# Rolled rows loaded with the 40 fields outermost, repeated rows written from SBUF, and k2 loaded last, in a DLRM tower on one core

## The reference, cut to what matters

```
e = stack([tbl_f[ids[:, f]] for f in range(40)], axis=1)      # (512, 40, 16)
x = e
for k in (k0, k1, k2):                                         # k0 (128, 40, 40), k1 and k2 (128, 128, 40)
    x = einsum('bhd,bmd,ohm->bod', x, e, k)                    # (512, 128, 16)
    outputs.append(sum(x, axis=-1))                            # (512, 128)
h = concatenate(outputs + [dense_ctx], axis=1)                 # (512, 384 + 16)
h = maximum(h @ W_top1 + b_top1, 0)                            # (512, 512)
h = maximum(h @ W_top2 + b_top2, 0)                            # (512, 256)
y = h @ W_top3                                                 # (512, 1)
```

## Time and profile before

| | |
|---|---|
| median of 3 runs | 780.76 us (780.18 to 788.1) |
| profiled execution | 787.09 us, of which the span of its instructions is 785.1 us |
| busy share, PE / DVE / ACT / POOL | 86% / 85% / 68% / 35% |
| mean granted TensorE clock | 0.972 |
| moved by DMA | 43.03 MB, 55 GB/s over the span |
| start of the first matmul on Y | 59.35 us |

### The profile page before, as it was taken

One profiled execution on the slowest core, in us unless ns is written; L12 is line 12 of the kernel. 1 busy time (PEld: TensorE's weight loads), 2 busy tenths in 40 slices (PEclk: granted clock), 3 DMA queues, 4 the chain that ended last, 5 costly groups with the idle time before them and its releaser, 6 DMA issues.

```text
span 785.1 us, 12097 instructions
## 1 busy us (share of the span) xinstructions
PE 672.4 (86%) x2558; PEld 479.5 (61%) x2558; DVE 670.2 (85%) x1607; ACT 530.8 (68%) x1753; POOL 274.8 (35%) x250
## 2 busy tenths in 40 slices
PE   0057998989888989898989999898989898987998
PEld 0025766666656767676756666666666676764483
DVE  3325999999979999999979999999999999999391
ACT  2204787868757777777766777786878687787293
POOL 6413244443533353535344444444353501010000
PEclk9997999999999999999989999999999999999699
DMA  6251212112211121212112111111211211100000
GB/s 193 58 183 56 60 63 48 59 53 56 57 53 45 41 63 51 58 44 66 45 55 45 64 46 62 47 57 52 60 52 48 61 50 55 51 1 28 0 1 1
DMA packets 45538, 43.03 MB, mean 55 GB/s; under 512 B 25615, under 2 KB 28943, under 8 KB 45216
## 3 DMA queue, kind: packets, MB, share of 16 engines
q1 hardware_dynamic: 40352, 41.07, 16.3%
q0 software_dynamic: 5120, 1.32, 2.7%
HBM read 41.06 MB, written 1.97 MB: 55 GB/s over the span
## 4 chain that ended last, share of the span: by engine, by line
PE 52%; DVE 25%; issue 10%; DMA 6%; ACT 3%; DVEq 2%; SPq 1%; POOL 1%; ACTq 0%
PE Y L610 10%; PE Y L612 10%; PE Y L611 10%; DVE sums L522 10%; PE X L577 7%; DVE sums L478 5%; DVE sums L483 5%; DMA pairs<-scratch 3%; PE GB L584 3%; DVE pairs_lo L455 3%; ACT sums L403 2%; DVE sums L469 2%; DMA scratch<-x0g 2%; PE X L571 2%; PE X L638 1%
## 5 line engine op out<-in xcount | busy, mean ns | idle before, releaser
L403 ACT ACTIVATE sums<-Y,xtok 128x128 f32<-128x128 f32 x1536 | 423.8, 380 | 125.8 <-PE Y L612 114.4
L610 PE MATMUL Y<-k1lo,x1hi 128*128 128x512 f32 x640 | 302.1, 472 | 29.6 <-DVE sums L522 22.0
L522 DVE SCALAR_TENSOR_TENSOR sums<-Y,xtok,sums 128x128 f32<-128x128 f32 x1024 | 285.8, 342 | 19.2 <-ACT sums L403 11.7
L611 PE MATMUL Y<-k1hi,x1hi 128*128 128x512 f32 x640 | 255.9, 400 | 0.0
L612 PE MATMUL Y<-k1hi,x1lo 128*128 128x512 f32 x640 | 255.7, 400 | 0.0
L338 POOL TENSOR_TENSOR diag<-xtok,mask 128x320 f32<-128x320 f32 x64 | 81.2, 1269 | 363.4 <-PE GB L584 363.2
L309 POOL DMA_INDIRECT x0g<-in_table,rows_now x160 | 189.3, 1183 | 42.2 <-issue 38.7
L610 PEld LDWEIGHTS Y<-k1lo,x1hi 128*128 128x128 f32 x640 | 122.2, 191 | 88.7 <-DVE sums L522 44.3
L611 PEld LDWEIGHTS Y<-k1hi,x1hi 128*128 128x128 f32 x640 | 122.8, 192 | 41.5 <-issue 14.4
L612 PEld LDWEIGHTS Y<-k1hi,x1lo 128*128 128x128 f32 x640 | 122.3, 191 | 30.3
L448 DVE TENSOR_TENSOR pairs<-pairs,A 120x512 f32<-120x512 f32 x112 | 76.6, 684 | 31.2 <-DMA pairs<-scratch 31.2
(11 more groups left out here) (74 smaller groups left out, 365.6 us busy)
## 6 DMA issues: line engine op xcount, KB each, us to landing
pairs<-scratch SPq DMA_DIRECT2D x112, 240.0 KB
A<-scratch SPq DMA_DIRECT2D x16, 240.0 KB
k1raw<-in_k SPq DMA_DIRECT2D x1, 2560.0 KB, 10.4
x0g<-in_table,rows_now POOLq DMA_INDIRECT x160, 3.8
k2s<-in_k SPq DMA_DIRECT2D x1, 2560.0 KB, 14.1
scratch<-x0g SPq DMA_DIRECT2D x64, 20.0 KB, 1.7
pairs<-in_w SPq DMA_DIRECT2D x3, 256.0 KB, 3.0
scratch<-scratch SPq DMA_DIRECT2D x16, 40.0 KB, 2.0
```

The costliest lines, as they stand in the source:

```text
L403: ins = nc.scalar.activation(sums[tile % 2][:, k * O:(k + 1) * O], Y[(NCH * tile + c) % YB][:, i * O:(i + 1) * O], ACT.Copy, scale=xtok[sl ...
L522: nc.vector.scalar_tensor_tensor(out=chain[tile % 2][:, i * O:(i + 1) * O], in0=Y[(NCH * tile + c) % YB][:, i * O:(i + 1) * O], scalar=xto ...
L610: nc.tensor.matmul(y, hi[:, tok], k1lo[:, cols], start=True, stop=False)
L611: nc.tensor.matmul(y, hi[:, tok], k1hi[:, cols], start=False, stop=False)
```

## The change

Three things are changed. First, the address pattern by which `A3` and `pairs` are loaded from `scratch` has the 40 fields outermost and the 3 shifts inside, instead of the other way round. A partition now is field x 3 + shift rather than shift x 40 + field; the host orders the rows of k0's weights accordingly, and `xtok` takes every third column of each token's transposed rows. Second, the rows 40 to 59 of `scratch` are written straight from `x0g` by two more transfers of 20 KB, in place of the copy of 40 KB in DRAM, and the wait between is gone. Third, SP issues the load of k2 behind its last group, not behind the first.

```
                 def rows(first, step):
                     return bass.AP(scratch.tensor, (par * ROLLS + first) * GROUP,
-                                   [[step * GROUP, KC], [GROUP, M], [1, GROUP]])
+                                   [[GROUP, M], [step * GROUP, KC], [1, GROUP]])
 
                 sp.wait_ge(s_gather[par], 16 * GF * (GPB // 2 * u + (slot + 1) // 2 + 1))
                 for q in range(FQ):
-                    sp.dma_start(scratch[par, q * GF:(q + 1) * GF, :].rearrange("f (b d) -> b f d", d=D),
-                                 x0g[par][q * GS:(q + 1) * GS, :, :]).then_inc(s_scratch, 16)
-                sp.wait_ge(s_scratch, 16 * FQ * (g + 1))
-                sp.dma_start(scratch[par, M:ROLLS, :], scratch[par, 0:ROLLS - M, :]).then_inc(s_again, 16)
-                sp.wait_ge(s_again, 16 * (g + 1))
+                    for first in range(q * GF, ROLLS, M):
+                        sp.dma_start(scratch[par, first:first + GF, :].rearrange("f (b d) -> b f d", d=D),
+                                     x0g[par][q * GS:(q + 1) * GS, :, :]).then_inc(s_scratch, 16)
+                sp.wait_ge(s_scratch, 16 * (ROLLS // GF) * (g + 1))
                 sp.dma_start(A3[par][0:PR, :], rows(0, 0)).then_inc(s_a3, 16)
...
             spread(0, -1)
-            sp.dma_start(k2s[:, :, :], k2.rearrange("h (m o) -> h m o", o=O)).then_inc(s_k2, 16)
-
             def body(u, last):
                 for slot in range(GPB - last):
                     spread(u, slot)
             over_groups(sp, body)
 
+            sp.dma_start(k2s[:, :, :], k2.rearrange("h (m o) -> h m o", o=O)).then_inc(s_k2, 16)
             sp.wait_ge(s_x1free, NG)
...
                     nc.scalar.activation(xtok[par][:, :, :], TR[:, 0:TPG * PR].rearrange(
-                        "p (j r) -> p j r", r=PR)[:, :, 0:M], ACT.Copy).then_inc(s_xtok, 1)
+                        "p (j m k) -> p j m k", m=M, k=KC)[:, :, :, 0], ACT.Copy).then_inc(s_xtok, 1)
...
     for k in range(KD):
-        k0a[k % KC, :, k // KC] = k0[h, (h + k) % M]
+        k0a[:, k % KC, k // KC] = k0[h, (h + k) % M]
         if 0 < k < KD - 1:
-            k0b[k % KC, :, k // KC] = k0[(h + k) % M, h]
+            k0b[:, k % KC, k // KC] = k0[(h + k) % M, h]
```

More of the change, by code:

```diff
@@ L208, in build @@
         s_xtok = sem("xtok_ready")
-        s_scratch, s_again, s_a3 = sem("scratch_written"), sem("scratch_repeated"), sem("a3_in")
+        s_scratch, s_a3 = sem("scratch_written"), sem("a3_in")
         s_roll = [sem(f"rolled_in{i}") for i in range(NR)]
@@ L679 @@
     h = np.arange(M)
-    k0a = np.zeros((KC, M, NC0, O), np.float32)
-    k0b = np.zeros((KC, M, NC0, O), np.float32)
+    k0a = np.zeros((M, KC, NC0, O), np.float32)
+    k0b = np.zeros((M, KC, NC0, O), np.float32)
     for k in range(KD):
-        k0a[k % KC, :, k // KC] = k0[h, (h + k) % M]
+        k0a[:, k % KC, k // KC] = k0[h, (h + k) % M]
         if 0 < k < KD - 1:
-            k0b[k % KC, :, k // KC] = k0[(h + k) % M, h]
+            k0b[:, k % KC, k // KC] = k0[(h + k) % M, h]
     ident, mask = constants()
```

## The result

The changed kernel took 759.8 us (758.94 to 760.03, 4 executions), the kernel before in the same set 784.43 (780.18 to 789.02, 4 executions). The ratio is 0.968, 95% interval 0.961 to 0.975: 3.2% faster. Repeated later with 6 executions beside 11 of the kernel before it was 759.9 against 781.56, ratio 0.970 (0.966 to 0.975). The forecast was 758.3 in a range of 752 to 767.

The account below looks back on a forecast made before the run. VectorE was taken to bound steady groups, leaving gains only at the start: 16.3 there plus 6.2 at group 1 gives 22.5 us, taking the median 780.76 to 758.3, range 752 to 767.

Parts of the forecast that it names:

- The bound: Steady groups: VectorE's own instructions set the 40.47 us period, loads cost nothing there, and groups stay at 40.5.
- Part 1: Start of group 0: forty fields outermost cut a load from 3.3 to 1.0 us; start gains 16.3, copy and k2 included.
- a chain of computing takes over from the loads: Group 0's start: with short loads, computing sets the time; product 0 at 27.6, first Y matmul at 43.0 us.
- xtok's stride: ScalarE reading every third element in PSUM: bounds 0 and 4.8 us per group, 0.3 at worst in group 0; taken as nothing.
- Part 2: SP's queue: copy's 2.07 us wait removed, two issues of 0.94 added; net 1.1 earlier, counted in group 0, hidden later.
- the price of small pieces: Scratch writes in 64-byte pieces: by the 512 B rule two more could cost about 1 us once, giving 21.5 gained.
- Part 3: k2 issued last: the 6.15 us wait at group 1's first product goes, gaining 6.2; no cost at the end.
- The sum: Whole kernel: 16.3 at the start plus 6.2 at group 1 gives 22.5 us, subtracted from the median 780.76.
- such a stall may come or not: Two loop edges: ScalarE's idle put down to issue, 10.3 us together, treated as occasional and left out of the gain.
- Rival 1: Loads not widened, descriptors still dealt three ways: only 9.3 us gained, giving 771.5; chance 0.05.
- Rival 2: TensorE granted clock 0.5 for all of group 0: 34 us over the period, giving 792.3; chance 0.03.
- Rival 3: More engines reading overlapping DRAM rows get worse than three: at 6 us a load, 113 us slower; chance 0.02.

Follow-up runs that it names:

- the kernel before with the move: Kernel before, with eight top-layer matmuls needing only z0 and the context put ahead of the last G on TensorE: 784.37 us.
- the pair with the move: Changed kernel and kernel before, each with eight top-layer matmuls put ahead of the last G: 755.16 and 784.37 us.
- the kernel with k2 and writes: Changed kernel with loads turned back to 3 shifts outermost, keeping k2 last and the two added writes: 777.64 us, 0.990 of the kernel before.

## Why the prediction was right, point by point

**The bound.** The steady group was set by VectorE and didn't move, 40.44 against 40.47. Right.

**Part 1, the width and the start.** A load takes 1.06 us; the forecast had 1.0. The first matmul on Y came at 41.91 where 43.0 was forecast, so 17.4 instead of 16.3. From the last matmul of chunks 0 to 2 to the product whose load waited for it took 3.5 to 3.8 us, where 3.5 was taken for the landing alone, so this term held. The two steps that were off: the A3 issue was at 21.68, not 22.25, since six writes from 17.41 landed in 4.27 us; and TensorE's rows had come to their higher level by 34.57, so that four matmuls take 2.25, where the forecast kept 2.99 from the earlier trace rows. TensorE then waits 0.65 and 0.70 us for products 5 and 6, so the landings decide the end of the chain. The reading that a chain of computing takes over from the loads is right in kind. Loads 4 to 6 remain in it with a wait of 1.1 us each. They were forecast to be on par with TensorE.

**xtok's stride** costs nothing: 304 ns against 303.

**Part 2.** By the last x1lo the writes gave 3.1 alone and 1.1 on top of k2's move (671.4 to 670.3), where 1.1 was forecast; both lie within the spread of that event. In group 0 A3's issue follows the first write by 4.27 us instead of 5.65, a gain of 1.4. Alone they also shorten the wait at group 1. The small pieces were no loss beside the copy: the writes' median time to landing stays 1.7 us, so the 1 us that the forecast gave as the price of small pieces did not show.

**Part 3.** Group 0 is 7.1 shorter, 6.2 of it forecast. Most of the rest, 0.7, is TensorE's clock at the first matmuls on Y. k2's move at the end cost nothing: it is issued at 634.3, lands in 8.8 us and is first read at 686.6.

**The sum** was 22.5, and 24.6 and 21.7 were measured by medians in the two sets. That it came so near is in part luck, as two errors cancel in it. The step that failed is "such a stall may come or not": the loop-edge waits belong to the three-wide loads and are worth 5.9 us, which the change gained beyond the forecast. Nor were these waits the 6.3 us between the profiled execution and the median: the kernels at 771 (span 769.2) and at 776.54 (the kernel before with the move) have both of them. What the 6.3 us were isn't shown. The stretch at clock 0.50 at the end is a part at most; in the profiled pair the end took 2.2 us more after the change, and no execution of the kernel before near 780 was profiled. Without the end, the change is worth 30.4 us in this pair of profiles and 29.2 in the pair with the move (678.6 to 649.4), while the medians of the kernels without the move show 24.6 and 21.7. This difference is only in part accounted for.

**The rivals.** Rival 1 (no widening) is what the kernel with k2 and writes is; its gain was priced at 9.3 and is 9.7 by the last x1lo, but 3.9 by its median (781.57 to 777.64). Rival 2 feared a lower clock in group 0; there it was granted 1.00 throughout (first windows above), more than the 0.85 before, which gave 0.7 us. The clock mattered more at the other end of the program. Rival 3 had no sign.

## What to carry to other kernels

Read the DMA share while a single transfer runs. Here a share near 3/16 stood beside an outermost dimension of 3, and 0.64 beside one of 40. Putting a larger dimension outermost is free if the order of partitions can be folded into the host's weights. The cost of a narrow load isn't only its own time: the narrow loads here were hidden in all steady groups and still cost 5.9 us, through another engine's wait at the loop edges. And when executions differ by 1% without a pattern, look at the granted clock at the end before explaining the difference by the change, and compare by an event ahead of it, knowing how far that event repeats (649.4 to 652.7 here).

## What the runs showed of the hardware that I had not expected

- A wait "<- issue" of 5 us on ScalarE behind a loop's branch follows the narrow traffic: twice in each of six profiles with it (five kernels with narrow loads and the one with narrow loads added), never in seven without. It ends 1.2 to 2.2 us after a packet of the instruction queue.
- In eleven of twelve profiles with a pause of TensorE of 1.7 to 4.5 us near the end, 6.8 to 23.9 us at granted clock 0.50 came during the pause or behind it, although TensorE was busy from the pause's end on. In the twelfth (1.73 us) 1.00 held. With the pause filled, 1.00 held in the profiled execution, and the median fell by 5.5 us (756.79 to 751.34).
- k2's 2.5 MB landed in 8.8 us at the end and in 14.1 behind the narrow loads of group 0.
